# A recurrent stage with its silus in halves and its norms a segment ahead, and causal attentions that split queries and keys straight from PSUM

## The reference

```python
# sublayer 1: four mamba blocks on each of two batch rows
for i in range(4):
    h = layer_norm(x, norm_w[i], norm_b[i])
    u, z = split(h @ in_w[i])                       # 512 + 512 channels
    u = silu(cb + sum(shift(u, k) * cw[:, k] for k in range(4)))
    dbl = u @ xw
    dt = softplus(dbl[..., :64] @ dtw + dtb)
    B, C = dbl[..., 64:80], dbl[..., 80:]           # 16 states
    h_t = exp(dt * A) * h_(t-1) + (dt * u) * B_t    # over all t, for 512 channels x 16 states
    y = sum_n(h_t * C_t) + u * D
    x = x + (y * silu(z)) @ ow
# sublayer 3 (causal attention and experts) and sublayer 4 (causal attention, gelu) both have
scores = q @ k.T ; masked to t' <= t ; softmax ; @ v      # 16 heads of 16
```

## Time and profile before

| what | value |
|---|---|
| time, median of 3 runs | 4773.03 us (4762.74 to 4781.94) |
| profiled execution, its own time | 4812.17 us |
| its span in the profile | 4810.5 us |
| recurrent stage | about 70 to 2070 us of the span |
| busy: PE, DVE, ACT, POOL | 4110.7, 3197.0, 2001.7, 2265.1 us |

### The profile page before, as it was taken

How to read it: one execution, slowest core, us unless ns; L and a number is a source line. 1 busy time by engine, 2 the same in 40 slices (tenths; PEclk the granted TensorE clock), 3 DMA queues, 4 the chain that set the end, 5 groups by cost and what they waited for, 6 DMA issues and landing times. The chain is left out here.

```text
span 4810.5 us, 50784 instructions
## 1 busy us (share of the span) xinstructions
PE 4110.7 (85%) x16032; PEld 2276.1 (47%) x16032; DVE 3197.0 (66%) x5216; ACT 2001.7 (42%) x3534; POOL 2265.1 (47%) x1928
## 2 busy tenths in 40 slices
PE   7888888888998888759858887999968999966998
PEld 2333333333333333224432336888833444655898
DVE  4999999999999999954466645444445554155433
ACT  5666566656565656432234451111112444222100
POOL 6888888888888888820021112444330111000320
PEclk9999999999999999979768898999977999988899
DMA  4555544554455544510062201000061320000000
GB/s 121 133 134 147 136 139 134 139 140 141 134 136 146 140 133 134 143 43 0 0 122 33 40 11 57 14 26 26 1 155 48 53 52 10 9 16 0 27 20 29
DMA packets 288996, 375.34 MB, mean 78 GB/s; under 512 B 100481, under 2 KB 131516, under 8 KB 288508
## 3 DMA queue, kind: packets, MB, share of 16 engines
q1 hardware_dynamic: 288764, 372.57, 30.4%
HBM read 343.80 MB, written 26.21 MB: 77 GB/s over the span
## 5 line engine op out<-in xcount | busy, mean ns | idle before, releaser
L521 POOL TENSOR_TENSOR arena<-arena 128x512 f32<-128x512 f32 x1024 | 1284.3, 1274 | 260.3 <-DVE psum L764 254.6
L764 DVE TENSOR_TENSOR_SCAN psum<-psum,arena 128x512 f32<-128x512 f32 x1024 | 1280.6, 1251 | 78.7 <-ACT psum L670 78.0
L871 PE MATMUL psum<-arena,base 128*128 128x512 f32 x2048 | 1083.9, 631 | 262.5 <-DVE arena L739 261.5
L670 ACT ACTIVATE psum<-arena 128x512 f32<-128x512 f32 x1024 | 699.5, 689 | 271.5 <-DVE arena L739 252.6
L871 PEld LDWEIGHTS psum<-arena,base 128*128 128x128 f32 x2048 | 348.5, 192 | 921.9 <-DVE arena L739 745.0
L739 DVE TENSOR_TENSOR arena<-psum,arena 128x512 f32<-128x512 f32 x1024 | 691.3, 675 | 0.0
L283 POOL TENSOR_TENSOR rounded<-arena,rounded 128x512 fp32r<-128x512 f32 (+2 forms) x181 | 315.9, 1751 | 791.8 <-DVE rounded L279 791.8
L289 PE MATMUL psum<-rounded 128*128 128x256 f32 (+1 forms) x1728 | 561.6, 325 | 33.1 <-DVE arena L1689 16.2
L290 PE MATMUL psum<-rounded 128*128 128x256 f32 (+1 forms) x1728 | 561.0, 325 | 0.0
L291 PE MATMUL psum<-rounded 128*128 128x256 f32 (+1 forms) x1728 | 560.3, 324 | 0.0
L1158 DVE TENSOR_REDUCE arena<-psum 128x1 f32<-128x512 f32 (+3 forms) x768 | 403.2, 555 | 199.6 <-PE psum L1221 139.1
(11 more groups left out here) (287 smaller groups left out, 5171.7 us busy)
## 6 DMA issues: line engine op xcount, KB each, us to landing
arena<-mb_bc_rows SPq DMA_DIRECT2D x512, 512.0 KB, 4.8
arena<-L_ffn_w SPq DMA_DIRECT2D x34, 512.0 KB, 4.4
arena<-f_parts SPq DMA_DIRECT2D x96, 128.0 KB, 6.5
arena<-l_parts SPq DMA_DIRECT2D x96, 128.0 KB, 6.4
l_v<-arena SPq DMA_DIRECT2D x16, 512.0 KB, 3.6
arena<-l_v SPq DMA_DIRECT2D x32, 256.0 KB, 4.4
f_parts<-arena SPq DMA_DIRECT2D x24, 256.0 KB, 2.4
l_parts<-arena SPq DMA_DIRECT2D x24, 256.0 KB, 2.4
```

What stands on the lines that cost most here:

```text
L521: eng.tensor_tensor(drive[:, u % RD, :], dtu[:, g % 2, m, :], bc_sb[:, v % RB, 0, :], ALU.mult)\
L670: eng.activation(ps[:, DECAY + u % ND, :], dt[:, g % 2, m, :], ACT.Exp, scale=a_neg[:, g // 4 % 2, m, n:n + 1]).then_inc(decay_ready, 1)
L764: eng.tensor_tensor_scan(state(u), state(u), drive[:, u % RD, :], first, ALU.mult, ALU.add).then_inc(scanned, 1)
L871: eng.matmul(ps[:, Y + u % 2, :], sh.ident, hc[:, u % RW, :], start=False, stop=n == NS - 1).then_inc(added_up, 1)
```

## The change

In the recurrent stage the places of the front's and the back's steps change, and three of them are cut up. The silu of z, one of 128x2048 at position 62 of the segment before, becomes two of 128x1024 at 22 and 34 of the segment itself, each behind the two silus of u of the next front, between the same two table loads. The out projection and the convolution are issued in halves, one half a position. The norm statistics, the normalization and the transposition of the front f+1 are made in segment f-1 instead of partly in segment f. In the attentions ACT makes the first and the second part, the first from PSUM (or the source) directly, DVE only the remainder; and SP issues the loads of the first two stacks between the stores of the tasks.

```diff
@@ mamba, scalar
-        def gate_z(f):
-            for m in range(M - 2, M):
+        def gate_z(f, half):
+            for m in (2 * half, 2 * half + 1):
                 wait_taken(eng, use(f, ZP + m))
-            eng.activation(sz[:, f % 2], sz[:, f % 2], ACT.Silu).then_inc(z_ready, 1)
-            exp_tables()
+            rows_z = sz[:, f % 2, 2 * half:2 * half + 2, :]
+            eng.activation(rows_z, rows_z, ACT.Silu).then_inc(z_ready, 1)
...
             if f + 1 < SEGS:
-                if p == 55:
+                if p == 29:
                     deviation(f + 1)
-                elif p in (58, 60, 62, 63):
-                    normalize(f + 1, (58, 60, 62, 63).index(p))
+                elif 36 <= p < 40:
+                    normalize(f + 1, p - 36)
+                elif p in (62, 63):
+                    rows(f + 1, p - 62)
+            if g == 0 and p in (0, 1):
+                rows(1, p)
+            if p in (22, 34):
+                if f < SEGS:
+                    gate_u(f, (p - 22) // 12)
+                gate_z(g, (p - 22) // 12)
+                exp_tables()
             if f < SEGS:
-                if p in (3, 5):
-                    rows(f, (p - 3) // 2)
-                elif p in (12, 14, 16, 18):
-                    copy_u(f, (p - 12) // 2)
-                elif p == 26:
-                    gate_u(f, 0)
-                elif p == 36:
-                    gate_u(f, 1)
...
+                if p in (4, 6, 8, 10):
+                    copy_u(f, (p - 4) // 2)
...
-                elif p in (55, 57, 59, 61):
-                    copy_z(f, (p - 55) // 2)
-                elif p == 62:
-                    gate_z(f)
+                elif p in (46, 48, 50, 52):
+                    step(f, (p - 46) // 2)
                 elif p in (47, 49, 51, 53):
...
+                    exponential(f, (p - 47) // 2)
+                elif p in (54, 56, 58, 60):
+                    copy_z(f, (p - 54) // 2)
@@ mamba, vector
             if f + 1 < SEGS:
-                if 50 <= p < 54:
-                    statistics(f + 1, p - 50)
+                if 23 <= p < 27:
+                    statistics(f + 1, p - 23)
...
-            if g > 0 and p in (8, 10):
-                add_out(g - 1, (p - 8) // 2)
+            if g > 0 and p in (13, 15):
+                add_out(g - 1, (p - 13) // 2)
@@ mamba, tensor
+            if f + 1 < SEGS and p in (59, 61):
+                turn(f + 1, (p - 59) // 2)
             if f < SEGS:
-                if p in (0, 2):
-                    turn(f, p // 2)
-                elif p in (9, 11, 13, 15):
-                    in_projection(f, 0, (p - 9) // 2)
-                elif p in (18, 20, 28, 30):
-                    convolve(f, (18, 20, 28, 30).index(p))
-                elif p == 38:
+                if p in (1, 3, 5, 7):
+                    in_projection(f, 0, (p - 1) // 2)
+                elif 14 <= p < 18:
+                    convolve(f, (p - 14) // 2, (p - 14) % 2)
+                elif 25 <= p < 29:
+                    convolve(f, 2 + (p - 25) // 2, (p - 25) % 2)
+                elif p == 37:
                     x_projection(f)
-                elif p in (42, 44, 46, 48):
-                    dt_projection(f, (p - 42) // 2)
-                elif p in (50, 52, 54, 56):
-                    in_projection(f, 1, (p - 50) // 2)
-            if g > 0 and p in (4, 6):
-                out_projection(g - 1, (p - 4) // 2)
+                elif p in (43, 44, 46, 48):
+                    dt_projection(f, (43, 44, 46, 48).index(p))
+                elif p in (51, 53, 55, 57):
+                    in_projection(f, 1, (p - 51) // 2)
+            if g > 0 and 9 <= p < 13:
+                out_projection(g - 1, (p - 9) // 2, (p - 9) % 2)
@@ causal_attention, write_parts
+    def early_stacks(eng, scratch):
+        eng.wait_ge(s["init"], 5)
+        for i in range(SLOTS - 1):
+            load_stacks(eng, scratch, i)
...
+            if n == early[0]:
+                for k in early[1]:
+                    eng.wait_ge(sent[k % SLOTS], (k // SLOTS + 1) * 48)
+                early[2](eng)
@@ self_attention, gelu_attention
-        wp["sync"](eng)
+        wp["sync"](eng, (3, (0, 1), lambda eng: att["early"](eng, scratch)))
...
-        wp["sync"](eng)
+        wp["sync"](eng, (5, (0, 4), lambda eng: att["early"](eng, parts_scratch)))
```

More of the change, by code:

```diff
@@ L651, in scalar @@
             copy_z(0, m)
-        gate_z(0)
         deviation(1)
@@ L834, in dt_projection, with out_projection @@
             eng.matmul(bank(k), w_dt[0:R, m * P:(m + 1) * P], dt_low[0:R, :], start=True, stop=True).then_inc(front_done, 1)
-        def out_projection(e, o):
+        def out_projection(e, o, t):
             k = use_out(e, o)
[L838 to L845, removed]
+            if t == 0:
+                eng.wait_ge(w_out_loaded, (e // 4 + 1) * 16)
+                eng.wait_ge(gated, (e + 1) * M)
+                wait_bank_free(eng, k)
+            for m in range(M):
+                mm = eng.matmul(bank(k)[:, t * D:(t + 1) * D], sz[:, e % 2, m, (2 * o + t) * P:(2 * o + t + 1) * P],
+                                w_out[:, m, :], start=m == 0, stop=m == M - 1)
+            if t:
+                mm.then_inc(front_done, 1)
         def skip_path(g, half, q):
@@ L858, in tensor @@
         for m in range(M):
-            convolve(0, m)
+            for part in range(2):
+                convolve(0, m, part)
         x_projection(0)
@@ L864, in tensor @@
             in_projection(0, 1, m)
+        for c in range(DC):
+            turn(1, c)
         for u in range(SEGS * UNITS):
@@ L1072, in rows @@
                     .then_inc(s["rows_in"], 16)
-        eng.wait_ge(s["init"], 5)
         stacks_wait(eng)
-        for i in range(SLOTS):
-            load_stacks(i)
+        load_stacks(eng, scratch, SLOTS - 1)
         v_wait(eng)
@@ L1385, in sync @@
                 eng.dma_start(dst, part[j][:, n % SLOTS, :]).then_inc(sent[n % SLOTS], 16)
-    n_proj = sum(t[3] is not None for t in tasks)
-    return (st, rest), [(sem, 48 * (N // SLOTS)) for sem in sent], {"taken": s["taken"], "sync": sync, "scalar": scalar, "vector": vector, "pool": pool, "tensor": tensor}
+            if n == early[0]:
+                for k in early[1]:
+                    eng.wait_ge(sent[k % SLOTS], (k // SLOTS + 1) * 48)
+                early[2](eng)
+    return (st, rest), [(sem, 48 * (N // SLOTS)) for sem in sent], {"taken": s["rest"], "sync": sync, "scalar": scalar, "vector": vector, "pool": pool, "tensor": tensor}
 def self_attention(sh):
```

135 lines of the change are left out of this document (73 added, 62 removed).

## The result

The changed kernel took 4853.61 us (median of four runs) against 4777.48 us before. One of the four runs, at a disturbed clock (5172 us), is left out of the ratio, 1.0153, 95% interval 1.0111 to 1.0195; the other three took 4840.82 to 4858.16, median 4849.06. The predicted range ended at 4848. So the change makes the kernel slower by 1.0 to 1.5%, by these ratios 46 to 73 us; 42 us were forecast.

The account below looks back on a forecast made before the run. DVE's waits were all the recurrent loop could give back. Loop +45, weights +18, prologue -4, attentions -10 and -6 gave +43: 4855 us profiled, x 0.992 = 4815 us; range 4750 to 4848.

Parts of the forecast that it names:

- copies of u: Recurrent loop, positions 4 to 10: DVE waits 2.08 us in an even segment, 1.36 in an odd one.
- weights: Start of segments 3, 7 and 11: PE waits 6.0 us each for late weights, +18 us.
- block at 22: Silu block at position 22 with z's silu added: DVE waits 2.38 us in even segments, 1.75 in odd.
- step to copies of z: Recurrent loop, about positions 46 to 60: new waits of 4.6 us in even segments, 2.05 in odd.
- distance rule: Recurrent loop: product-to-copy distance of 3 positions costs about 1.0 us, 2 about 2.7, 4 nothing.
- Less 112.7: +46: Recurrent loop: new DVE waits of 159 us less the 112.7 now there give +46, taken as +45.
- prologue: Before the loop: the silu of z leaves ACT's chain, -4 us.
- The attentions: Both causal attentions: earlier stack loads save 10 us in the first and 6 in the second.
- B: Recurrent loop: step and z stretch does not wait; no change, -6 us, 4767; chance 0.22.
- C: Recurrent loop: removed waits count in full, new distances don't bite; -63 us, 4710; chance 0.16.
- D: Segment starts: weights land before PE asks; 4797, inside the main case's range, no chance of its own.
- E: Attentions: their loads bring nothing; +16 us, 4831, inside the main case's range, no chance of its own.

Follow-up runs that it names:

- weights early: Changed kernel with the next block's weights loaded one unit pair earlier and the in projection waiting for its own weights alone; ratio 1.0063 to before.
- distance two: Changed kernel with the copies of u two positions behind their in projections instead of three; 5038.99 us, one time.
- distance four: Changed kernel with products issued four positions ahead of their ACT steps (the second transposition three); ratio 0.9986 to before.
- all mended: Changed kernel with distances of four, earlier weights, and x projection, residual adds, first convolutions and first silu block at other positions; 4700.23 us, ratio 0.9851 to before.
- attentions alone: Kernel before with only the changed attentions; ratio 0.9915 to before.
- V first: All mended, with V's stores ahead of the third stack's loads in the second attention and first convolutions at 15 to 18; 4700.41 us, ratio 0.9797 to before.
- run on parts: Kernel before with the attentions' new parts, but the first stacks' loads issued after all of the tasks' stores; ratio 0.9979 to before.
- longer measurement: The changed kernel measured again as it is, in more rounds; 4830.49 us against 4782.21 before, ratio 1.0097.

## Why the prediction was right and where it was wrong

**The direction and the mechanism were right.** DVE's waits were forecast at 159 + 18 = 177 us in the loop and measured at 182.1, of which 2.7 are the wait before the loop's first scan. By place, over the segments:

| place | forecast | measured |
|---|---|---|
| copies of u, without the weights | 26.2 | 39.0 (in weights early) |
| weights | 18 | 24.5 (what weights early has less there) |
| residual adds | 20.9 | 17.1 |
| block at 22 | 31.3 | 30.5 |
| step to copies of z | 51.2 | 43.7 |
| segment end | 28.3 | 19.7 (without the loop's first scan) |
| gates | 1.5 | 4.9 |

So it is partly luck that the sum came so near: 23 us too little at the copies of u, the weights and the gates stand against 21 too much elsewhere. The distance rule was read from segment 6, and the 0.92 us before scan 17, which the prediction calls an agreement, belongs to the copy that it was read from. The runs test it elsewhere: at three positions scans 9 and 47 wait 0.92 in even and 0.59 to 0.60 in odd segments (forecast 0.92 and 0.97 in even ones), at two 2.63 and 2.37 where the clock is full (forecast 2.7), at four, the weights aside, hardly any wait is left but the one before scan 42.

**The step that failed is the sum**: "Less 112.7: +46" for the loop, and with the weights +18 and the prologue -4. It prices a wait at its idle time alone. The loop's own length grew by 78.2 us, where the terms gave 45 + 18 = 63; the prologue was right (the first scan starts at 66.1 instead of 70.9). Of the 15 us, 5 are more of idle (2.7 of them the wait before the first scan, which is in the 112.7 and not in the 159) and 1 was rounded off. The largest, 9, is that a wait costs more than its idle time: back to back, DVE's instructions overlap (scan 13 starts at 850.91 and lasts 1.23, scan 14 starts at 852.64, and a weighting of 0.67 stands between: 1.90 us of work in 1.73), 0.08 to 0.09 us for each of the two. A scan that waits loses one such overlap. The changed kernel has 211 waits in the loop and the one before 100; 111 x 0.09 = 10 us. The loop less its waits is 1894.4 and 1885.6 us, 8.8 apart. With distance two, where 244 waits add up to 356.7 us, it is 1897.6, and with distance four, where 115 waits add up to 116.2 us, 1885.6 again; with 68 waits in all mended it falls no further (1885.8).

**The copies of u** were 13 us short, as their price was taken from rows of position 13, where PE runs at full clock. At positions 1 to 5 it often does not. In segment 4 of the changed kernel, as a window from the first scan on, and in segment 6:

```profile
586.40:596.00 9.60, 7.05 (x9) 2.82 (x10) 9.60 (x12) 2.74 (x5) 9.52 (x8) 0.65 0.42 112
596.00:610.00 14.00, 13.41 (x31) 5.37 (x30) 9.43 (x12) 6.57 (x16) 13.84 (x12) 1.00 0.38 112
...
847.40:857.00 9.60, 6.72 (x15) 2.73 (x16) 9.60 (x12) 2.71 (x5) 9.52 (x9) 1.00 0.36 115
```

In segment 4 the granted clock is 0.65 for the first 9.6 us and 1.00 after, in segment 6 it is 1.00 from the start. Scan 5 waits 3.65 us in the one and 1.24 in the other; in segments 1, 5, 8, 9 and 13, at 0.82, it waits 1.70 to 1.95. In the kernel before such slow matmuls stood at the segment's start too, in segment 8 four matmuls of its adds that took 3.54 us, where four at the loop's end (2069.93) took 1.98:

```profile
1074.91 3.54 PE L871 MATMUL psum<-arena,base 128*128 128x512 f32 x4 [2.15 <-DVE arena L739]
```

There ACT waited only for the transpositions so early, at 3 and 5, which cost DVE 6.1 us before scan 4 over all segments; the in projection came at 9.

**The weights** were right: 18 forecast, 20.7 won back; the wait itself was 5.2 us a time instead of 6.0, and the matmuls at half clock behind it made up for it.

**The attentions** (-16) were about right in size, 10 to 13 us at equal clock in the run of the attentions alone. In the profiles, the mean lengths in the table of the eight executions with the whole change (without V first) against those of the two without it, 506.5 against 519.0 and 726.8 against 733.6, leave 12.5 and 6.8 us, where single executions of the first scatter by 23. In the second the reason was wrong, as the run on parts shows.

**The range** ended 6 us below the first median of four and 1 us below that of the three. With the loop's 15 us in the sum the forecast would have been 4830, 57 us above before, and the range would have held that time. That the longer measurement gave 4830.49 is luck: it is 48 us above its own kernel before, and its interval, 33 to 59 us, holds the 42 that were forecast and the 57 alike. The rest of the first one's 73 us goes with the clock of its runs, as told above. Scaling the profiled execution by 0.992 treated a stage that stood at its longer length as if every stage were slower; it moved the sum by little, since the forecast stood on the median.

Of the rivals, B (the z stretch does not wait) falls: it waits 43.7 us. C needed the distances not to bite; with the places mended they don't. That this run gives 4700, near the 4710 of C, is luck, since it has the weights early too. D falls with PE's wait of 15.6 us for A_log, and E in the first attention, where the early loads take the 9.0 us that the parts alone leave; in the second these loads brought nothing. On the rule of the Trainium skill, page ScalarE: Activation LUTs, section What ACT_TABLE_LOAD costs (2.66 us a switch, by which, as an estimate, 30 switches less would have won 80 us of ACT's time): the silu at 890.40 follows its load of 1.28 us at once, here as before. No drain shows, so that a switch is 1.28 us here.

## What to carry to other kernels

Where several engines run fixed orders, count for each product how many steps of the bounding engine lie between its issue and its use, and measure from the trace how many it needs; here four were enough, three cost up to about 1 us a place and two 2.4 to 2.7, more where TensorE's clock was low. Before a step is moved earlier, ask for everything that it waits for, its weights' loads in the queue too, and at which clock its engine runs there. Add the lost overlap to each new wait, and don't scale a profile to a median before you know which stage makes the difference. Before two medians of few runs are compared, look at the granted clock of each run.

## What the hardware showed that was not expected

An unchanged stage has two lengths, 243 to 245 and 267.5 us, by TensorE's granted clock (0.95 to 0.96 and 0.86), in executions of any of these kernels. What decides it stays open. Within the loop, waits of PE of 2 to 5.5 us were often followed by matmuls at half speed: behind the 5.50 us wait four took 3.78 us instead of 1.88, at a granted clock of 0.50 (464.4 to 468.3 us), the lower of the two levels (1.2 instead of 2.4 GHz). Not always: a wait of 1.96 us at the segment's start had slow matmuls behind it in segment 4 and full speed in segment 6, and what decides that is not shown. The Trainium skill, TensorE: Matmul & The Clock Gate, Part 1, has the throttled state as the default and activity as what releases it; the rows behind the 5.50 us wait agree.
